# Attention loop of a small vision tower: ScalarE lays the upper halves of every eighth tile of probabilities side by side, and that tile's wide sums read the copy

## The reference

```
f = l2norm(h)                       # 8192 x 64
scores = f @ f.T                    # 8192 x 8192
attn = softmax(scores, axis=-1)
feats_att = attn @ f
h = layernorm(h + l2norm(0.8 * f + 0.2 * feats_att))
```

## Time and profile before

| | |
|---|---|
| median of 3 runs | 859.27 us (858.8 to 859.43) |
| the profiled execution's own time | 861.66 us |
| its span (first to last instruction) | 858.2 us |
| TensorE busy | 841.4 us, 98% |
| VectorE busy | 776.7 us, 91% |
| ScalarE busy | 658.4 us, 77% |
| GpSimd busy | 184.2 us, 21% |
| mean granted TensorE clock | 0.997 of full speed |
| attention loop | about 70 to 757 us of the span |

### The profile page before, as it was taken

One profiled execution on the slowest core, in us unless ns is written; L12 is line 12 of the kernel. 1 busy time (PEld: TensorE's weight loads), 2 busy tenths in 40 slices (PEclk: granted clock), 3 DMA queues, 4 the chain that ended last, 5 costly groups with the idle time before them and its releaser, 6 DMA issues.

```text
span 858.2 us, 31358 instructions
## 1 busy us (share of the span) xinstructions
PE 841.4 (98%) x13604; PEld 435.0 (51%) x13604; DVE 776.7 (91%) x916; ACT 658.4 (77%) x1309; POOL 184.2 (21%) x191
## 2 busy tenths in 40 slices
PE   8999999999999999999999999999999999999995
PEld 6544556755555555555555555555555555543331
DVE  3588999999999999999999998999989999999994
ACT  0168887887888788878887888788788788977873
POOL 1085820000400000000000000000000299948323
PEclk9999999999999999999999999999999999999998
DMA  9994140000000000000000000000000000000111
GB/s 270 347 214 85 21 86 12 3 3 2 3 2 2 3 3 3 3 3 3 2 3 3 2 3 3 3 2 2 3 2 3 3 2 3 3 2 2 38 26 37
DMA packets 31592, 26.06 MB, mean 30 GB/s; under 512 B 12568, under 2 KB 29472, under 8 KB 31456
## 3 DMA queue, kind: packets, MB, share of 16 engines
q1 hardware_dynamic: 22880, 15.40, 7.6%
q10 hardware_dynamic: 8512, 8.66, 3.5%
q0 software_dynamic: 64, 0.01, 0.0%
HBM read 17.77 MB, written 2.10 MB: 23 GB/s over the span
## 4 chain that ended last, share of the span: by engine, by line
PE 92%; DVE 4%; ACT 2%; issue 1%; DMA 0%; POOLq 0%; DVEq 0%; POOL 0%; ACTq 0%
PE ps L565 38%; PE ps L582 27%; PE ps L595 13%; PE ps L667 3%; PE ps L749 3%; PE ps L474 1%; PE ps L450 1%; ACT ring L967 1%; PE ps L609 1%; DVE ring L1261 1%; PE ps L679 1%; PE ps L488 1%; PE ps L462 1%; PE ps L478 1%; DVE sums L1053 1%
## 5 line engine op out<-in xcount | busy, mean ns | idle before, releaser
L1096 DVE TENSOR_TENSOR ring<-ring 128x1024 f16<-128x1024 f32 x512 | 605.0, 1232 | 33.2 <-ACT ring L967 32.2
L967 ACT ACTIVATE ring<-ps 128x1024 f32<-128x1024 f32 x512 | 519.2, 1020 | 121.2 <-PE ps L565 120.9
L565 PE MATMUL ps<-big 64*64 64x512 f16 x6144 | 376.1, 375 | 1.3 <-ACT ring L967 0.9
L582 PE MATMUL ps<-ring,both_f 64*64 64x512 bf16 x4096 | 275.2, 384 | 0.0
L565 PEld LDWEIGHTS ps<-big 64*64 64x64 f16 x6144 | 176.6, 106 | 160.3 <-ACT ring L967 5.5
L582 PEld LDWEIGHTS ps<-ring,both_f 64*64 64x64 f16 x4096 | 119.3, 106 | 106.6
L595 PE MATMUL ps<-ring,both_f 64*64 64x512 f16 x2048 | 154.3, 376 | 0.1
L967 ACT ACTIVATION_READ_ACCUMULATOR ring<-ps 128x1 f32 x512 | 101.3, 198 | 0.0
L393 POOL TENSOR_SCALAR stat<-stat 128x16 f32<-128x16 f32 (+2 forms) x4 | 2.9, 723 | 444.1 <-DVE stat L1145 443.8
L595 PEld LDWEIGHTS ps<-ring,both_f 64*64 64x64 f16 x2048 | 59.7, 107 | 51.9 <-issue 1.9
L930 ACT ACTIVATE ring<-ps,b1s 128x512 f32<-128x512 f32 x64 | 40.4, 682 | 17.0 <-PE ps L667 17.0
(11 more groups left out here) (192 smaller groups left out, 563.6 us busy)
## 6 DMA issues: line engine op xcount, KB each, us to landing
ring<-in_x_dram SPq DMA_DIRECT2D x6, 1024.0 KB, 18.9
ring<-in_x_dram ACTq DMA_DIRECT2D x6, 1024.0 KB, 14.4
big<-big SPq DMA_DIRECT2D x16, 128.0 KB, 2.4
out_dram<-h SPq DMA_DIRECT2D x14, 128.0 KB, 2.4
both_f<-in_x_dram SPq DMA_DIRECT2D x1, 1024.0 KB, 24.2
both_f<-in_x_dram ACTq DMA_DIRECT2D x1, 1024.0 KB, 22.3
big<-in_x_dram SPq DMA_DIRECT2D x1, 1024.0 KB, 24.0
big<-in_x_dram ACTq DMA_DIRECT2D x1, 1024.0 KB, 14.2
```

Of the source, the lines that this page charges most:

```text
L565: last = mm(bank(SLOT_BANK[slot_of(s)] + r)[m:m + 64, :], of_k[r][:, 128 * k + m:128 * k + m + 64], of_q[r][:, q0 + 512 * r:q0 + 512 * r + ...
L582: last = mm(bank(sums_bank(s // NT) + half)[m:m + 64, :], fs[64 * r:64 * r + 64, s % NT, m:m + 64], probs[64 * r:64 * r + 64, s % 8, :].bi ...
L967: a(probs[:, s % 8, :], bank(SLOT_BANK[slot_of(s)], 2), ACT.Exp, accum_out=rowsum[:, s:s + 1]).then_inc(s_pr, 1)
L1096: tt(probs_lo[:, s % 8, :], probs[:, s % 8, :], probs[:, s % 8, :].bitcast(BF16)[:, 1:2 * QC:2], ALU.subtract).then_inc(s_lo, 1)
```

## The change

ScalarE makes, behind the Exp of every tile with s % 8 == 3 (64 of 512 tiles), a copy of the 1024 upper halves into a new contiguous bf16 buffer `upper` with two slots. It first waits for its own Exp (`s_pr`). The matmuls of the high sums for that tile, straight and crossed, read the copy; the other tiles are read as before. `high_sums` has a new wait ahead of the group, `s_upper >= g // 2 + 1`: a group with even g holds such a tile as its last (s = 4g + 3).

```diff
+        upper = sb("upper", [128, 2, QC], BF16)
+
+        def high_of(s, rows, half):
+
+            if s % 8 == 3:
+                return upper[rows, s // 8 % 2, 512 * half:512 * half + 512]
+            return probs[rows, s % 8, :].bitcast(BF16)[:, 1024 * half + 1:1024 * half + 1024:2]
...
             def high_sums(g, crossed):
                 pe.wait_ge(s_pr, 4 * g + 4)
+                pe.wait_ge(s_upper, g // 2 + 1)
...
-                                      probs[64 * r:64 * r + 64, s % 8, :].bitcast(BF16)[:, 1024 * half + 1:
-                                                                                       1024 * half + 1024:2],
+                                      high_of(s, slice(64 * r, 64 * r + 64), half),
...
                 a(probs[:, s % 8, :], bank(SLOT_BANK[slot_of(s)], 2), ACT.Exp,
                   accum_out=rowsum[:, s:s + 1]).then_inc(s_pr, 1)
+                if s % 8 == 3:
+                    act.wait_ge(s_pr, s + 1)
+                    a(upper[:, s // 8 % 2, :], probs[:, s % 8, :].bitcast(BF16)[:, 1:2 * QC:2], ACT.Copy).then_inc(s_upper, 1)
                 if q >= 1 and k % 2:
                     beside(q, k // 2)
```

More of the change, by code:

```diff
@@ L262, in tower @@
              "s_var2", "s_istd2", "s_fin", "s_out"))
-        s_w2c, s_last = sem("s_w2c"), sem("s_last")
+        s_w2c, s_last, s_upper = sem("s_w2c"), sem("s_last"), sem("s_upper")
         s_ch = [sem(f"s_ch{i}") for i in range(3)]
```

## The result

The changed kernel takes 877.31 us (877.25 to 877.73, three runs) against 859.27: a ratio of 1.020, 95% interval 1.019 to 1.022. It is slower by 18.0 us; 20.7 were forecast. The profiled execution's span is 875.2 us against 858.2, 17.0 longer.

A forecast was written before the change was run, and what follows sets the result against it. TensorE bounds the attention loop, with ScalarE's Exps just ahead. Stalls from 64 copies, less saved rounds, summed by class of place to 20.7 us; added to the 859.27 us median: 879.9 us, range 871 to 889.

The forecast's parts named there:

- parts 2 and 3: ScalarE in the attention loop: copy waits 0.04 us for its own Exp; later Exps late, TensorE stalls 0.28 us per copy.
- part 1: 64 copies on ScalarE, every eighth of 512 tiles, behind an odd Exp: 1.056 us each, bounds 0.63 and 1.9.
- part 4: TensorE's high sums: two rounds per copy read without stride, saving 0.022 us each copy, 1.4 us over 64.
- the last rival: Stall absorbed by the slack behind ScalarE's hole, saved rounds stand: at best -1.4 us, 857.9 us; chance 0.02.
- Weight loads waiting: Sign in TensorE's waits for ScalarE's Exps: some 50 of 0.5 to 0.6 us, near 30 us instead of 1.9.
- part 5: TensorE's new wait for the copy ahead of the high sums: covered by 0.2 us, costs nothing.
- part 6: VectorE gets two tiles 0.5 us late, needs 2.46 of 2.63 us per step; costs nothing.
- Other side: Faster case, chance 0.02: a copy of 0.79 us or less ahead of ScalarE's even Exp is swallowed by the slack.

## Why the prediction was right, point by point

- *Bound and mechanism* (parts 2 and 3): right. The loop is TensorE's with ScalarE just ahead, and the price of a copy is lateness against a due time. The timeline above has each link: copy 0.03 behind the readout, next Exp 0.47 late (0.49 forecast), weights 0.225 late (0.245), step 2.87 (2.91 forecast). The run that kept the copies and took away ScalarE's wait for itself lowered the price by 0.15 us a place, the one that halved the copy's length brought it to zero at ordinary places.
- *Length of the copy* (part 1): 1057 ns for 1056. The stride cost ScalarE nothing that shows. The estimate from the Trainium skill (ScalarE: Activation LUTs, What ACT_TABLE_LOAD costs), 1.04 us, was 0.02 short; the rows extended from 256 and 512 elements were exact.
- *Saved rounds* (part 4): the 0.011 us is the stride's, as taken; with all tiles packed every round is 0.216. On this the measurement differs from the note on cachelines in the Trainium skill (SBUF — State Buffer), by which a stride of two bf16 elements would be free. But the term was wrong in its sum. I booked 0.022 us per copy, 1.4 in all; it was 0.9, because the straight round is saved ahead of the stall and lost in it. And without copies and stalls the packed round in the last place of its group brought nothing at all. Had the copies been free, the change as it stands would still have gained nothing; the saving that the last rival counted on, 1.4 us at best, was not there.
- *The size*: 20.7 us for the loop, 18.9 measured, 9% too much. Two terms were over-sized, and their errors partly cancel. The stalls were forecast at 20.7 + 1.4 = 22.1 us and are 19.9 in the run that has nothing else; the saving was forecast at 1.4 and is 0.9. In the stall I took 0.04 us for the self-wait where it was 0.03, and 0.03 for what is lost behind a late load where it was 0.025, with a lateness rounded up: 0.02 to 0.03 us a place, over 54 paid places 1.1 to 1.6 of the 2.2 us. Most of the rest is block 0, where the second place cost 0.19 and not 0.48. The whole execution grew by 18.0 us where the loop grew by 18.9; no term of the sum stands for that, and the starts of the loop differ by more than that between traces.
- *Weight loads waiting*: some 50 waits and 30 us forecast, 110 and 46.5 us found. The even tile's loads wait too (0.20 us at 327.88) at no cost, 44 times, about 9 us together. The other 66 wait 0.46 to 0.87 us each, 38 us together; places with other ScalarE work mostly have two of them. I had looked for one costly wait a copy only; the total of a wait row counts all.
- *The new wait on TensorE* (part 5) and *VectorE* (part 6): covered, as forecast. TensorE waited 0.3 us in all for the copy, and without the wait ahead of each group the loop was no shorter; VectorE has more idle time than before.
- *Other side*: the threshold of 0.79 us for a copy was right in kind: 0.63 us cost nothing at ordinary places, 1.06 us cost 0.25, and no length between was run. Even at 0.63 us the doubly loaded holes left a loss of 3.3 us, where +3 was forecast.

## What to carry to other kernels

On a side engine (one that is not the bound) that is "busy 77%", ask not how much idle time it has but how long its single hole is and what is due behind it: 68 us of copies in 1.06 us pieces cost 19 us, 107 us of them in pieces of 0.63 cost nothing. Cut side work to the length of the hole, let it read what is long finished, so that it does not wait for its own engine's last result, and leave out the places that are already loaded. And test the gain by itself before paying for it: here the short rounds were real and the loop was no shorter for them.

## What was unexpected of the hardware

A round of four matmuls side by side is 0.227 us when it reads bf16 at every second element and 0.216 when it reads them packed. With one packed round as the last of four (followed by scores), later strided rounds took 0.233 to 0.236 us, and steps that were 2.630 us became 2.640; with it as the first of four they did not. The same slow rounds stand in the trace of before, 31 of them, 20 of these in the second and third step behind the interlude of line 609 in five blocks, and 85 of them in the run with copies whose matmuls all read with the stride. A matmul whose weights came late started within 0.003 us of its weight load, and the round behind the stall took 0.24 instead of 0.216: 0.024 us more, and that is what the stall cost beyond the lateness.
